# Residual in place in the image buffer, tokens as whole rows, one quarter later

## The chip, the core and the metric

The kernel runs on one core of a Trainium2 chip. The metric is the time of one execution on the device in microseconds, the median of three runs. Five engines work side by side, each with its own instruction stream: TensorE (PE in the profile; PEld is its weight load), VectorE (DVE), ScalarE (ACT), GpSimd (POOL) and SyncE (SP), which here only starts DMAs. They wait for each other through semaphores.

## What is computed

Input x has 32 images of 96 channels and 56 by 56 pixels. A clustering attention is added to x, and a quantised feed-forward network (FFN) is added to that.

```python
x = x + conv_ref(layernorm_over_channels(x), ...)
t = to_tokens(x)                       # one token per pixel, 96 channels
t = t + ffn_ref(layernorm(t), W1, b1, W2, b2)
x = from_tokens(t, x)
```

Attention works on 28 by 28 quarters of an image (a fold of 2 by 2) and 8 heads. In each quarter 16 centers are pooled, every pixel goes to its most similar center, and the centers' aggregates are spread back and projected. The FFN has 384 hidden units with sign-valued weights. Its activations are scaled by the largest absolute value of a group of six images, once for the hidden layer and once for the output. Five groups make 30 images; the last two get attention and a zero FFN output.

## The kernel before

The unit of work is the quarter: 784 pixels in seven tiles of 112. Each group of six images has 24 quarters (`GQ`). For a group the program first runs a pipeline over the quarters (attention, the token layer norm, the hidden layer for its maximum only), then a second pass (`second_pass`) that computes the FFN with the known scale. The final addition of the FFN output to the stored tokens waits for the group's second scale, so it runs during the pipeline of the next group (steps tagged `FINAL`), or in the last, short pipeline for group 4.

`pipeline` (L213) writes the same kind of list for every engine: a stage letter, a lag of 0 or 1, and a step. One round of the list is a **slot**. A stage letter is the number of quarters that the stage runs ahead: x statistics and normalisation (`X`), features and scores (`M`), assignment and output of the attention (`A`), tokens and final additions (`R`). Lag 1 means that the step runs one slot after its stage began. Since the list is written out by hand, it alone sets the order on each engine. Slots ahead of quarter 0 exist only in the first group; in all others the next group's first quarters are handled in the last slots of the group before. The last part runs over the eight quarters of images 30 and 31; its `scaled` and `finish` do three quarters of group 4 in each slot.

Data on this path:

- `xbuf` has four buffers, each one half of an image (28 rows of 56 pixels) as read from `x`. `image_rows` (L253) gives a quarter of it: 28 rows of which each has 28 of 56 numbers. Buffer j holds quarters 2j and 2j+1, side by side.
- `gather` (L498) on ScalarE copies an x quarter into `xq`.
- `residual` (L754) on VectorE adds the attention's output in PSUM, the bias and the x quarter, and writes to the staging buffer `tq` (two quarters).
- `to_tokens("t", 6)` (L900) on TensorE transposes the seven tiles of `tq`; `stats("t", 6)` follows on VectorE, `moments("t", ...)` on GpSimd.
- `place_t` (L506) on ScalarE copies `tq` over the x quarter in `xbuf`, so that SP can store whole half images.
- `scaled` (L805) multiplies a quarter of FFN output, and `finish` (L815) clips it and adds it to the stored tokens, which SP has read back into `fin` (two half images).
- On SP, `body` (L312) does for each half image: store of the previous group's final half, store of this group's half, wait for it, load of x, wait for the final store, load of the next `fin`.

`marks` (L448) on GpSimd marks the best center of every pixel; it follows `maxima` (L717) on VectorE. `newton` (L421) on GpSimd makes the inverse norms that `cosine` (L710) needs.

## Time and profile before

| | us |
|---|---|
| runs | 3263.29, 3264.39, 3267.81 (median 3264.39) |
| span of the profiled execution | 3259.8 |
| TensorE busy | 2986.8 (92%) |
| VectorE busy | 2731.3 (84%) |
| ScalarE busy | 2271.4 (70%) |
| GpSimd busy | 2034.3 (62%) |

The profiled execution is one run of the program; its span goes from its first to its last instruction and lies 4.6 us under the median. Durations below come from it. "Busy" sums the instructions of an engine, whether or not anybody waited for them; the chain of work follows the last instruction back through whatever released it.

### The profile page before, as it was taken

Reading aid. Unit: us, or ns where it says so; the run is one execution under the profiler, and the core shown is the slowest. Engines: PE = TensorE matmul, PEld = TensorE weight load, DVE = VectorE, ACT = ScalarE, POOL = GpSimd, SP = SyncE. Lnnn points to the kernel's source line nnn. Section 1 sums busy time; section 2 is a strip of 40 time slices with the busy share of each in tenths; the row PEclk is TensorE's granted clock in tenths of the full one; section 3 lists DMA queues with packets and bytes.
Section 4 is the critical chain, followed back from the end, with each engine's and each line's share of the span. In section 5 each row is a group of like instructions: output and inputs, shape, how many; then the busy total and the mean of one; then the engine's idle time right before and its main releaser. Section 6 shows DMA issues by size and latency. Waiting matters only on the chain.

```text
span 3259.8 us, 72165 instructions
## 1 busy us (share of the span) xinstructions
PE 2986.8 (92%) x20760; PEld 2046.0 (63%) x20760; DVE 2731.3 (84%) x5896; ACT 2271.4 (70%) x4628; POOL 2034.3 (62%) x4668
## 2 busy tenths in 40 slices
PE   3999999989999988999998989999988999998985
PEld 2677776666666655666665566666655666665553
DVE  3788887989988987998887978888887889897966
ACT  1677676967776787777676967767686767677943
POOL 1676675256766755777675757766655777675743
PEclk9999998999999989999998989999988999998977
DMA  1011111012222200222221012222200222120024
GB/s 47 16 31 39 38 33 31 0 45 61 61 65 57 60 16 16 61 61 68 58 64 38 0 47 68 64 58 67 60 2 16 68 68 71 52 68 23 15 72 122
DMA packets 31010, 155.43 MB, mean 48 GB/s; under 512 B 6483, under 2 KB 6676, under 8 KB 30612
## 3 DMA queue, kind: packets, MB, share of 16 engines
q1 hardware_dynamic: 30612, 150.74, 16.7%
q8 instruction: 174, 2.85, 0.4%
q14 instruction: 224, 1.84, 0.2%
HBM read 76.06 MB, written 74.66 MB: 46 GB/s over the span
## 4 chain that ended last, share of the span: by engine, by line
POOL 40%; PE 24%; issue 22%; ACT 7%; DVE 6%; POOLq 1%; ACTq 0%; DVEq 0%; SPq 0%
PE ps L958 5%; POOL eq L452 5%; POOL mo_x L397 4%; PE ps L1033 4%; POOL mo_t L397 4%; ACT turns L588 3%; PE ps L1071 3%; POOL nxy L428 3%; POOL ninv L434 3%; POOL ny L426 3%; POOL mo_x L390 2%; POOL nxy L431 2%; POOL turns L468 2%; PE ps L922 2%; PE ps L966 2%
## 5 line engine op out<-in xcount | busy, mean ns | idle before, releaser
L958 PE MATMUL ps<-wfT,xn 97*112 97x384 f32 x1792 | 734.8, 521 | 39.5 <-issue 21.5
L1033 PE MATMUL ps<-tok,w1T 98*128 (+1 forms) x2880 | 615.1, 338 | 31.8 <-ACT turns L591 29.2
L532 ACT ACTIVATE sq<-ps 112x384 f32<-112x384 f32 x896 | 432.5, 490 | 212.6 <-PE ps L958 208.4
L784 DVE TENSOR_REDUCE hmax<-ps 128x392 f32 (+1 forms) x720 | 394.7, 561 | 72.3 <-PE ps L1033 63.1
L468 POOL CAST turns<-turns 128x392 f16<-128x392 f32 x240 | 319.6, 1348 | 209.2 <-ACT turns L588 200.2
L1033 PEld LDWEIGHTS ps<-tok,w1T 98*128 98x128 f16 x2880 | 282.9, 100 | 236.7 <-issue 54.8
L958 PEld LDWEIGHTS ps<-wfT,xn 97*112 97x112 f32 x1792 | 268.1, 181 | 250.0 <-ACT sq L532 82.0
L704 DVE TENSOR_REDUCE n<-sq 112x32 f32<-112x1536 f32 (+1 forms) x256 | 394.0, 1539 | 13.6 <-issue 8.5
L493 ACT ACTIVATE xnT<-ps,mo_x 112x96 f32<-112x96 f32 x896 | 305.2, 456 | 66.5 <-POOL mo_x L399 66.5
L855 DVE SCALAR_TENSOR_TENSOR turns<-turns 128x1176 f16<-128x1176 f32 x240 | 333.9, 1391 | 0.0
L538 ACT ACTIVATE sig<-cosb,betac 112x896 f32<-112x896 f32 x128 | 133.6, 1044 | 280.1 <-DVE cosb L714 280.0
L493 ACT ACTIVATE nT<-ps,mo_t 112x96 f32<-112x96 f32 x840 | 284.8, 439 | 59.4 <-POOL mo_t L399 48.6
L588 ACT ACTIVATE turns<-ps,scale 128x1176 f32<-128x1176 f32 x240 | 312.8, 1303 | 9.1 <-PE ps L1033 4.8
L1071 PE MATMUL ps<-turns,w2T 128*96 128x392 f16 x1440 | 292.5, 341 | 22.9 <-DVE turns L855 20.1
L452 POOL TENSOR_TENSOR eq<-sig,top 112x896 bf16<-112x896 f32 x128 | 219.8, 1717 | 116.2 <-issue 61.0
L966 PE MATMUL ps<-Q,xn 97*112 97x128 f32 x1792 | 240.5, 288 | 48.7 <-issue 25.5
L922 PE MATMUL ps<-cst,xnT 112*97 112x128 f32 x1792 | 254.5, 284 | 17.6 <-ACT xnT L493 17.6
L922 PEld LDWEIGHTS ps<-cst,xnT 112*97 112x97 f32 x1792 | 219.7, 168 | 66.3 <-ACT xnT L493 47.6
L966 PEld LDWEIGHTS ps<-Q,xn 97*112 97x112 f32 x1792 | 212.9, 184 | 68.1 <-ACT sq L532 36.9
L1071 PEld LDWEIGHTS ps<-turns,w2T 128*96 128x96 f16 x1440 | 164.2, 125 | 136.4 <-DVE turns L855 53.1
L998 PE MATMUL ps<-sim,xnT 112*97 112x128 f32 x1792 | 229.5, 281 | 2.4 <-ACT turns L554 2.3
L776 DVE TENSOR_TENSOR tok<-ps,tok 98x448 f32 (+1 forms) x240 | 135.8, 566 | 109.9 <-ACT tok L565 103.5
(130 smaller groups left out, 6369.3 us busy)
## 6 DMA issues: line engine op xcount, KB each, us to landing
xbuf<-in_x SPq DMA_DIRECT2D x64, 588.0 KB, 4.7
out<-xbuf SPq DMA_DIRECT2D x64, 588.0 KB, 3.7
turns<-out SPq DMA_DIRECT2D x60, 588.0 KB, 6.2
out<-turns SPq DMA_DIRECT2D x60, 588.0 KB, 3.7
cst<-in_constants SPq DMA_DIRECT2D x1, 644.0 KB
tok<-in_L_ffn_W SPq DMA_DIRECT2D x2, 142.5 KB
wf<-in_L_conv_Wf SPq DMA_DIRECT2D x1, 144.0 KB
tok<-in_L_conv_Wv SPq DMA_DIRECT2D x1, 144.0 KB
```

What stands on the lines that cost most here:

```text
L452: nc.gpsimd.tensor_tensor(heads(eq[:, :]), heads(sig[:, k % 2, :]), over_centers(top[:, :]), ALU.subtract)\
L468: nc.gpsimd.tensor_copy(ghi[:, k % 3, HT:2 * HT], gel[:, k % 3, HT:2 * HT]).then_inc(b_mid, 1)
L493: ins = nc.scalar.activation(dst, bank(b0 + part, TN, C, (t - t0) * C), ACT.Identity, bias=m[:, 9, t:t + 1], scale=m[:, 8, t:t + 1])
L532: nc.scalar.activation(sq[:, t, :], bank(2 + t % 2, TN, D), ACT.Square).then_inc(f_sq, 1)
L588: nc.scalar.activation(gel[:, k % 3, :].rearrange("p (c n) -> p c n", c=FC), ps[:, h:h + 3, 0:HT], ACT.Gelu, scale=scale[:, 0:1]).then_inc ...
L704: ins = v.reduce_sum(n2[:, t0 * HEADS:t1 * HEADS], sq[:, t0:t1, :].rearrange("p t (h d) -> p (t h) d", d=HD), AX.X)
L784: v.tensor_reduce(o, bank(6 + u % 2, 128, HT), AX.X, ALU.max, apply_absolute_value=True)\
L922: ins = mm(bank(part, C + 1, BN, (t - t0) * BN), xnT[:, k % 4, t, :], backm[:, t, :], start=True, stop=True)
L958: mm(bank(2 + t % 2, TN, D), xn[:, k % 2, t * TN:(t + 1) * TN], wfT[:, :], start=True, stop=True)\
L966: ins = mm(tile_bank(2, TN, HM, t), xn[:, k % 2, t * TN:(t + 1) * TN], Q[:, k % 2, :], start=True, stop=True)
L1033: ins = mm(dst, w1T[:, c * 128:(c + 1) * 128], tok[:, bass.ds(place, 1), part, s * HT:(s + 1) * HT].rearrange("p a n -> p (a n)"), start=p ...
L1071: ins = mm(bank(6 + k % 2, C, HT), w2T[:, c, :], part[:, s, c * HT:(c + 1) * HT], start=n == 0, stop=n == 2 * FC - 1)
```

## The change

`residual` writes its sum to the place in `xbuf` from which it read x. `tq`, `place_t` and the semaphore `t_placed` are gone, and with them the waits of `residual` for the copy and for the transposes of two quarters before. The transposes read `xbuf`: token quarter k is no longer the 28 by 28 square of the attention but 14 whole rows of the half image, 784 consecutive numbers. Such a quarter needs both squares of its half, so `to_tokens` waits for the residual of the odd quarter in both cases, and the stages X, M and A run one quarter further ahead (4, 3, 2). The FFN output has the same token order, so `finish` adds consecutive numbers too. SP stores a half when its residual is done, and loads the next x over it when it has been transposed as well.

```diff
-        X, M, A, R = 3, 2, 1, 0
+        X, M, A, R = 4, 3, 2, 0
@@ SP, body
-                    done(sp, "t_placed", g * GQ + b * BODY + (2 * j + 1))
+                    done(sp, "t_done", g * GQ + b * BODY + (2 * j + 1))
                     store(image, j)
                     sp.wait_ge(t_out[j], (g * BODIES + b) * 16 + 16)
                     sp.sem_inc(waited, 1)
+                    done(sp, "t_T", g * GQ + b * BODY + (2 * j + 1))
                     load(x_half, image + XB // 2, j)
@@ ScalarE, attention
-                        (X, 1, normalise("x", 0, 1)), (R, 1, place_t), (X, 1, copy_x(0)), (X, 1, copy_x(1)),
+                        (X, 1, normalise("x", 0, 1)), (X, 1, copy_x(0)), (X, 1, copy_x(1)),
@@ VectorE, residual
-                    if half == 0:
-                        done(dve, "t_placed", q - 2)
-                        if part != "last":
-                            done(dve, "t_T", q - 2)
                     o = bank(4 + half, C, hi - lo).rearrange("c (r w) -> c r w", w=QS)
-                    t = tq[:, k % 2, lo:hi].rearrange("c (r w) -> c r w", w=QS)
-                    ins = v.scalar_tensor_tensor(t, o, bpc[:, :], image_rows(k, lo // QS, (hi - lo) // QS), ALU.add, ALU.add)
+                    t = image_rows(k, lo // QS, (hi - lo) // QS)
+                    ins = v.scalar_tensor_tensor(t, o, bpc[:, :], t, ALU.add, ALU.add)
@@ VectorE, finish
-                    t = fin[:, k // 2 % 2, :].rearrange("c (r w) -> c r w", w=SIDE)[:, :, k % 2 * QS:(k % 2 + 1) * QS]
-                    v.scalar_tensor_tensor(t, y_of(place).rearrange("c (r w) -> c r w", w=QS), -QCLIP, t,
-                                           ALU.max, ALU.add).then_inc(S["final"], 1)
+                    t = fin[:, k // 2 % 2, k % 2 * QN:(k % 2 + 1) * QN]
+                    v.scalar_tensor_tensor(t, y_of(place), -QCLIP, t, ALU.max, ALU.add).then_inc(S["final"], 1)
@@ TensorE, to_tokens
-                        done(pe, "t_done", q)
+                        done(pe, "t_done", q + 1 - k % 2)
                         pe.wait_ge(h_max, q * (2 * FC) + START)
                     for t in range(T):
-                        src = (xq if s == "x" else tq)[:, k % 2, t * TN:(t + 1) * TN]
+                        if s == "x":
+                            src = xq[:, k % 2, t * TN:(t + 1) * TN]
+                        else:
+                            src = xbuf[:, k // 2, k % 2 * QN + t * TN:k % 2 * QN + (t + 1) * TN]
```

How VectorE comes from `cosine` to the maxima in a full slot. First before: `tq` is the target of the residual, and the semaphores that an instruction waits for stand in brackets.

```order
L714 TENSOR_TENSOR cosb<-ps,ninv 112x896 [waits s_sig_done,s_n_newton3,s_s_ps]
L678 TENSOR_TENSOR cbd<-ps,cst 96x128 [waits s_q_ps,s_cen_f]
L765 SCALAR_TENSOR_TENSOR tq<-ps,bpc,xbuf 96x448 [waits s_t_T,s_t_placed,s_o_ps0]
L784 TENSOR_REDUCE hmax<-ps 128x1 [waits h_ps]
L765 SCALAR_TENSOR_TENSOR tq<-ps,bpc,xbuf 96x336 [waits s_o_ps]
```

The same stretch after the change:

```order
L708 TENSOR_TENSOR cosb<-ps,ninv 112x896 [waits s_sig_done,s_n_newton3,s_s_ps]
L672 TENSOR_TENSOR cbd<-ps,cst 96x128 [waits s_q_ps,s_cen_f]
L755 SCALAR_TENSOR_TENSOR xbuf<-ps,bpc,xbuf 96x16x28 [waits s_o_ps0]
L774 TENSOR_REDUCE hmax<-ps 128x1 [waits h_ps]
L755 SCALAR_TENSOR_TENSOR xbuf<-ps,bpc,xbuf 96x12x28 [waits s_o_ps]
```

The instructions stand in the same order; the target is `xbuf` in rows of 28, and two waits are gone.

The end of VectorE's stream, the last slots of the last part. Before: `rden` to `aggp` and the residual L765 belong to the last quarter's attention, L811 is the scaling, L821 the final addition.

```order
L738 RECIPROCAL rden<-ps 128x1 [waits s_a_ps]
L742 TENSOR_SCALAR hmul<-cst,rden 128x2 [waits s_a_rden]
L746 TENSOR_SCALAR a<-ps,hmul 128x96 [waits s_a_mul]
L751 SCALAR_TENSOR_TENSOR aggp<-ps,hmul,a 128x96 [waits s_o_ps,s_a_half]
L765 SCALAR_TENSOR_TENSOR tq<-ps,bpc,xbuf 96x448 [waits s_t_placed,s_o_ps0]
L765 SCALAR_TENSOR_TENSOR tq<-ps,bpc,xbuf 96x336 [waits s_o_ps]
L811 TENSOR_SCALAR tok<-tok,scale 96x784 x3
L821 SCALAR_TENSOR_TENSOR turns<-tok,turns 96x28x28 [waits s_c_min]
L821 SCALAR_TENSOR_TENSOR turns<-tok,turns 96x28x28 [waits s_c_min,f_in1]
L821 SCALAR_TENSOR_TENSOR turns<-tok,turns 96x28x28 [waits s_c_min]
```

After (L801 is the scaling, L811 the final addition):

```order
L755 SCALAR_TENSOR_TENSOR xbuf<-ps,bpc,xbuf 96x16x28 [waits s_o_ps0]
L755 SCALAR_TENSOR_TENSOR xbuf<-ps,bpc,xbuf 96x12x28 [waits s_o_ps]
L801 TENSOR_SCALAR tok<-tok,scale 96x784 x3
L811 SCALAR_TENSOR_TENSOR turns<-tok,turns 96x784 [waits s_c_min,f_in1]
L811 SCALAR_TENSOR_TENSOR turns<-tok,turns 96x784 [waits s_c_min]
L811 SCALAR_TENSOR_TENSOR turns<-tok,turns 96x784 [waits s_c_min,f_in0]
L801 TENSOR_SCALAR tok<-tok,scale 96x784 x3
L811 SCALAR_TENSOR_TENSOR turns<-tok,turns 96x784 [waits s_c_min]
L811 SCALAR_TENSOR_TENSOR turns<-tok,turns 96x784 [waits s_c_min,f_in1]
L811 SCALAR_TENSOR_TENSOR turns<-tok,turns 96x784 [waits s_c_min]
```

The last residual now stands ahead of six final additions instead of three; `f_in0` and `f_in1` are the loads of the two `fin` buffers.

The start of TensorE's stream, from the spread of the first quarter's attention (L1016, after it L1008) to the marks' transposes (L975, after it L967). Before:

```order
L1016 MATMUL ps<-turns,aggp 96x336 [waits s_a_done]
L958 MATMUL ps<-wfT,xn 112x384 [waits s_xn_copied0,s_cos_done]
L938 MATMUL ps<-cst,csq 128x1 [waits s_cen_sq,s_cen_bd]
L941 MATMUL ps<-wf,cbd 32x97 x4
L958 MATMUL ps<-wfT,xn 112x384
L911 MATMUL ps<-cst,tq 112x96 [waits h_max,s_t_done]
L911 MATMUL ps<-cst,tq 112x96 x6
```

After:

```order
L1008 MATMUL ps<-turns,aggp 96x336 [waits s_a_done]
L950 MATMUL ps<-wfT,xn 112x384 [waits s_xn_copied0,s_cos_done]
L930 MATMUL ps<-cst,csq 128x1 [waits s_cen_sq,s_cen_bd]
L933 MATMUL ps<-wf,cbd 32x97 x4
L950 MATMUL ps<-wfT,xn 112x384
L950 MATMUL ps<-wfT,xn 112x384 [waits f_sq] x2
L939 MATMUL ps<-cst,qT 97x128 [waits s_q_scaled]
```

The token transposes are missing in this slot and come one slot later, from `xbuf`.

## Rows read from the trace of the kernel before

**Rows 1.** Chain of work, middle slots of group 1: start us, us, what.
```profile
795.25 1.71 POOL eq L452
...
814.46 1.72 POOL eq L452
...
831.22 0.67 DVE tq L765
...
832.37 0.47 DVE tq L765
```

**Rows 2.** Timeline of one middle slot: start us, us, engine, line, operation [idle before].
```profile
807.02 0.86 ACT L509 COPY xbuf<-tq 96x784 f32<-96x784 f32 x1
...
808.83 0.44 ACT L522 COPY xn<-ps 97x336 f32<-97x336 f32 x1 [0.53 <-PE ps L922]
...
810.50 1.09 DVE L714 TENSOR_TENSOR cosb<-ps,ninv 112x896 f32<-112x896 f32 x1 [0.59 <-issue]
...
812.77 0.56 DVE L765 SCALAR_TENSOR_TENSOR tq<-ps,bpc,xbuf 96x336 f32<-96x336 f32 x1
...
813.73 0.74 PE L911 MATMUL ps<-cst,tq 96*112 96x96 f32 x7
```

**Rows 3.** Timeline of VectorE, first slots: the x statistics.
```profile
92.34 1.25 DVE L661 BATCH_NORM_STATS2 st_x<-ps 112x6 f32<-112x96 f32 x7
...
110.74 1.25 DVE L661 BATCH_NORM_STATS2 st_x<-ps 112x6 f32<-112x96 f32 x7 [0.20 <-PE ps L911]
...
129.17 1.25 DVE L661 BATCH_NORM_STATS2 st_x<-ps 112x6 f32<-112x96 f32 x7 [0.20 <-PE ps L911]
```

**Rows 4.** Timeline of VectorE, last part: final additions of slots three to eight.
```profile
3149.26 2.73 DVE L821 SCALAR_TENSOR_TENSOR turns<-tok,turns 96x784 f32<-96x784 f32 x3
...
3175.18 2.73 DVE L821 SCALAR_TENSOR_TENSOR turns<-tok,turns 96x784 f32<-96x784 f32 x3
...
3196.58 2.73 DVE L821 SCALAR_TENSOR_TENSOR turns<-tok,turns 96x784 f32<-96x784 f32 x3
...
3216.82 2.73 DVE L821 SCALAR_TENSOR_TENSOR turns<-tok,turns 96x784 f32<-96x784 f32 x3
...
3235.98 2.73 DVE L821 SCALAR_TENSOR_TENSOR turns<-tok,turns 96x784 f32<-96x784 f32 x3
...
3245.64 1.69 DVE L811 TENSOR_SCALAR tok<-tok,scale 96x784 f32<-96x784 f32 x3
3247.25 2.73 DVE L821 SCALAR_TENSOR_TENSOR turns<-tok,turns 96x784 f32<-96x784 f32 x3
```

**Rows 5.** Timeline of SP's queue, last part: issues of DMAs.
```profile
3227.78 0.32 SPq L301 DMA_DIRECT2D turns<-out  x1
...
3248.24 4.04 SPq L306 DMA_DIRECT2D out<-turns  x2
3255.69 0.32 SPq L297 DMA_DIRECT2D out<-xbuf  x1
```

**Rows 6.** Groups of instructions: busy us, mean ns of one, idle before and releaser.
```profile
L855 DVE SCALAR_TENSOR_TENSOR turns<-turns 128x1176 f16<-128x1176 f32 x240 | 333.9, 1391 | 0.0
...
L765 DVE SCALAR_TENSOR_TENSOR tq<-ps,bpc,xbuf 96x448 f32<-96x448 f32 (+1 forms) x256 | 156.4, 613 | 2.0 <-PE ps L1016 2.0
...
L821 DVE SCALAR_TENSOR_TENSOR turns<-tok,turns 96x784 f32<-96x784 f32 x120 | 113.9, 959 | 0.0
L509 ACT COPY xbuf<-tq 96x784 f32<-96x784 f32 x128 | 110.6, 864 | 6.8 <-DVE tq L765 6.8
```

**Rows 7.** Timeline of GpSimd, last part: an instruction beneath three final additions.
```profile
3149.30 2.77 POOL L390 TENSOR_SCALAR mo_x<-mo_x 112x7 f32<-112x7 f32 x1
```

**Rows 8.** From 3175 us on: landing of the six `fin` loads, then of eight final stores.
```profile
DMA to landing us min/median/max: 4.4/4.6/4.7
...
DMA to landing us min/median/max: 3.6/3.7/5.8
```

**Rows 9.** The page's first line.
```profile
span 3259.8 us, 72165 instructions
```

More of the change, by code:

```diff
@@ L504, in gather @@
                     .then_inc(S["x_side"], 1)
-            def place_t(k, q, place, use):
-                done(act, "t_done", q)
-                nc.scalar.copy(image_rows(k), tq[:, k % 2, :].rearrange("c (r w) -> c r w", w=QS))\
-                    .then_inc(S["t_placed"], 1)
             def copy_x(part):
@@ L752, in second_heads, with residual @@
                     .then_inc(S["a_done"], 1)
-            def residual(half, part):
+            def residual(half):
                 _, _, lo, hi, end = BANKS[half]
@@ L832, in attention @@
                          (R, 1, h_largest(2, 3), FFN), (A, 1, second_heads), (R, 1, h_largest(3, 5), FFN),
-                         (X, 1, pooled), (M, 1, cosine), (X, 1, centers), (A, 1, residual(0, part)),
-                         (R, 1, h_largest(5, 6), FFN), (A, 1, residual(1, part)), (X, 1, center_floor),
+                         (X, 1, pooled), (M, 1, cosine), (X, 1, centers), (A, 1, residual(0)),
+                         (R, 1, h_largest(5, 6), FFN), (A, 1, residual(1)), (X, 1, center_floor),
                          (A, 0, maxima), (X, 1, q_scaled), (R, 0, stats("t", 6), FFN),
```

5 lines of the change are left out of this document (2 added, 3 removed).

## The prediction, made before the change was run

> **What bounds the kernel now.** I read the chain of work first, then the timeline of one slot of a middle group, then the two ends of the program. A slot is one round of the hand-written order, which each engine runs once per quarter of an image. In a middle group the slots follow each other every 19.21 us: GpSimd's `marks` starts at 795.25 and again at 814.46 [rows 1]. Between them the chain stays on GpSimd until its third Newton step ends; VectorE takes over at 810.50 with `cosine` [rows 2] and keeps it for 4 us: the centers, the two halves of the residual with one `h_largest` between them (831.22 and 832.37 in the next slot, [rows 1]), the maxima, and then GpSimd again. So GpSimd and VectorE close a ring. TensorE is the busiest engine but not on it, and neither is ScalarE. 96 of the 120 full slots are of this kind. In group 0, where no final additions run, a slot takes 18.43 us (110.74 to 129.17, [rows 3]). At the end, eight slots carry the last eight quarters together with the 24 outstanding final additions, three in each [rows 4], and a run of DMAs closes the program [rows 5].
>
> **The staging copy.** ScalarE loses 128 copies of 864 ns, 110.6 us of its busy time [rows 6]. In a middle slot the copy stands at 807.02, before the two copies of xn; the second of those then waits 0.53 us for TensorE until 808.83 [rows 2]. The removed 0.86 us becomes idle time in front of a copy that TensorE releases. What hides it is the x-back matmuls, and nothing of it is on the ring: 0. Were that cover gone, it would be worth up to the 110.6 us; the wait at 808.83 excludes that.
>
> **The residual in place.** This is the one edited instruction on the ring, twice per slot. It reads strided rows of the image buffer already and now writes them too, 28 of every 56 numbers. It takes 613 ns on average for a mean of 392 elements [rows 6]. No such instruction of before writes so from PSUM; the nearest is the final addition L821, which reads and writes strided rows: 959 ns for 784 elements, 1.22 ns each. The contiguous L855 takes 1391 ns for 1176, 1.18 ns each [rows 6]. If all of that difference were the stride it would be 3%, 0.02 us an instruction, 0.04 us a slot, 4 us over 96 slots; since a shorter instruction carries more fixed time per element, I take 0 and keep 4 us to each side. The two waits that leave it (for the copy and the transposes of two slots before) were long met: 0.
>
> **The wait of the transposes.** For an even quarter `to_tokens` now waits for the residual of the next quarter. That residual is computed in the same slot, since its lead grew by one, so the event comes at the same place: VectorE ends it at 813.33, TensorE begins at 813.73 [rows 2]. Behind the wait on TensorE stand the feature matmuls and, through them, ScalarE's squares; with a margin of 0.4 us nobody waits. Odd quarters find their residual done a slot ago, but TensorE gets to them in its own order and no earlier. 0 for both.
>
> **Final additions on whole rows.** The same elements, now contiguous: 959 ns stays, down to 927 by L855's rate. While L821 runs, GpSimd stands: in the last stage one small GpSimd instruction lasts 2.77 us [rows 7] beneath three of them at 3149.26 [rows 4]. [...]
>
> **SP's queue.** In middle groups SP waited for ScalarE's copy, one slot after the final addition; now the x store goes out right behind the final store, and the next load waits for the transposes, which precede that addition on VectorE. A store lands after 3.7 us, 5.8 at most, a load after 4.6 [rows 8]: some 12 us together, and the gather needs them two slots (38 us) later. Behind SP's new wait stand only the next half's DMAs. 0.
>
> **The pipeline is one slot deeper.** The leads go from 3, 2, 1 to 4, 3, 2. In middle groups this only renames quarters. At the start there is one more slot of attention before the FFN begins. X statistics start at 92.34, 110.74 and 129.17 [rows 3]; the new slot has the work of the one from 92.34 to 110.74, 18.40 us, without its seven token transposes (0.74 us on TensorE, [rows 2]). The feature matmuls behind those also wait for ScalarE's squares, so I take nothing off: **+18.4 us**, lower bound 17.7.
>
> At the end one slot of full attention goes. The first three periods have the same work in both kernels, so the one that goes is the fourth, 3175.18 to 3196.58: **-21.4 us** [rows 4]. Its three final additions do not go; they land in a last slot that has nothing else. Call T the start of the additions in the slot before the one with the last residual. Before, T = 3235.98; the last slot starts its own at T+11.27, its first is done at T+12.2 [rows 4], and three stores in series from 3248.24 to 3255.69 and 3.7 us more [rows 5] end at T+23.8. After, T lies in the sixth slot. In the seventh the third addition needs an input half whose load goes out 10.96 us after T (3227.78 against 3216.82, [rows 4, 5]) and lands 4.6 us later [rows 8]: it runs from T+15.6 to T+16.6. Three scalings (1.69 us together, [rows 4]) and the first addition of the eighth slot end at T+19.2. The store of half 9 could go at T+13.2 but stands behind a load and a store of x, so I estimate its landing at T+18.6; the last input half is there at T+23.3, two additions end at T+25.2, the last final store at T+29.0, the last x store at T+32.8, the program at **T+33.2**: **+9.4 us**. Bounds: +4.3 if no load were late (first addition T+16.5, then the same 11.6); +14 if every transfer on the way took 5.8.
>
> **The sum.** 18.4 - 21.4 + 9.4 = **+6.4 us**. The profiled execution spans 3259.8 us [rows 9]; the median of the runs, 3264.39, is 4.6 above it. That makes a span of 3266.2 and a median of 3270.8, 0.20% more. A measurement of this kernel can tell about 0.2% (6.5 us) from no change, so the forecast lies just inside that line.
>
> **The rivals.**
> *Shorter slots (faster).* Fewer ScalarE instructions and fewer waits on VectorE draw 0.15 us out of each ring: -14.4 + 6.4, so 3256.4. For it: the ring has gaps of some tenths between instructions; against: none of them lies at an edited wait. Chance 0.1, and half of it at smaller gains.
> *Whole rows make the final addition faster.* The scaling of a whole quarter takes 0.56 us when GpSimd is silent (1.69 for three, [rows 4]). If L821 did as well, GpSimd would be free 0.40 us earlier in 96 slots: -38 us, 3232.4. L855, contiguous and with two inputs, speaks against it with 1.18 ns an element. The Trainium skill (VectorE: DVE Perf Modes, The perf-mode tier table) gives two-tensor fp32 instructions only the single rate; the trace agrees. Chance 0.02.
> *The last loads hold up one more slot (slower).* If final additions wait for input in the sixth slot as well, a load's 4.6 us is added: 3275.4. It decides as soon as two sets of additions follow within the 15.6 us that a store and a load take. Periods of 19 us and more speak against it before the seventh slot. Chance 0.18.
> *The clock at the end.* The third period took 25.92 us instead of 21.4 (3149.26 to 3175.18, [rows 4]). If the shortened end loses or gains such a slot, it moves 4.5 us: 3266.3 or 3275.3. Chance 0.2, split evenly.
>
> **How the numbers follow.** The forecast itself keeps 0.5; 0.17 of that lies past the 0.2% line, since its own unknowns are some 4 us to each side. Slower by over 0.2%: 0.18 + 0.1 + 0.17 = 0.45. Faster by over 0.2%: 0.08 of the first two rivals, the rest of them falls within. Within: 0.47. The range goes from 3260, where the small gains of the first rival end, to 3276, past the two slower rivals.
>
> **What would show it.** In the profile after, ScalarE is some 110 us less busy, and two `marks` of a middle slot stay 19.2 us apart. The first FFN matmul comes 18.4 us later. In the last stage seven slots carry attention, the last two sets of final additions wait for loads, and SP's last stores no longer stand back to back. A middle slot that is off by 0.1 us moves the whole by 10 us and breaks the forecast, and so would a residual above 0.65 us on average.

## The result: 22 us faster, where 6 us slower was predicted

| | before, same chip | after |
|---|---|---|
| median of four runs | 3266.03 | 3243.77 |
| runs | 3263.29 to 3267.81 | 3240.04 to 3246.68 |
| span of the profiled execution | 3259.8 | 3244.8 |

The ratio of the runs is 0.9934, with a 95% interval of 0.992 to 0.9948. The predicted range began at 3260. The sign was wrong. The profiled execution of the changed kernel was its slowest run (3246.68), so the two spans differ by 15.0 us only; the stretches below are taken from them.

The page of the changed kernel, its first lines:

```profile
span 3244.8 us, 71952 instructions
...
PE 2979.5 (92%) x20760; PEld 2041.8 (63%) x20760; DVE 2709.1 (83%) x5896; ACT 2176.7 (67%) x4500; POOL 1858.7 (57%) x4668
```

ScalarE is 95 us less busy, near the 110 of the copy. Part of the rest is in the second passes, where its activations are recorded longer (L588 before, L582 after: 1303 and 1497 ns on average) though they follow each other no more slowly. GpSimd lost 176 us, though the change does not touch one instruction of it. That is the first thing that the prediction has no term for.

The lines that answer to [rows 1], chain of work of the changed kernel in the middle slots of group 1 (start us, us, what), two `marks` of neighbouring slots:

```profile
796.37 1.71 POOL eq L452
815.59 1.72 POOL eq L452
```

They stand 19.22 us apart, as in [rows 1]. Timeline of the same slot, the lines that answer to [rows 2]: residual (L755, L765 before) and token transposes (L903, L911 before).

```profile
812.83 0.67 DVE L755 SCALAR_TENSOR_TENSOR xbuf<-ps,bpc,xbuf 96x448 f32<-96x448 f32 x1
813.89 0.56 DVE L755 SCALAR_TENSOR_TENSOR xbuf<-ps,bpc,xbuf 96x336 f32<-96x336 f32 x1
...
814.86 0.74 PE L903 MATMUL ps<-cst,xbuf 96*112 96x96 f32 x7
```

The residual ends at 814.45 and the transposes begin 0.41 us later, as before. By the page of the changed kernel, stores from `xbuf` land after 5.7 us instead of 3.7 and final stores after 4.4 instead of 3.7; no slot got longer by it. The groups of instructions that answer to [rows 6], and three of the second pass (busy us, mean ns of one):

```profile
L844 DVE SCALAR_TENSOR_TENSOR turns<-turns 128x1176 f16<-128x1176 f32 x240 | 333.4, 1389 | 0.0
...
L755 DVE SCALAR_TENSOR_TENSOR xbuf<-ps,bpc,xbuf 96x448 f32<-96x448 f32 (+1 forms) x256 | 156.4, 613 | 1.6 <-PE ps L1008 1.6
L468 POOL CAST turns<-turns 128x392 f16<-128x392 f32 x240 | 143.3, 597 | 367.4 <-ACT turns L582 358.5 <-PE ps L1063 8.9
...
L811 DVE SCALAR_TENSOR_TENSOR turns<-tok,turns 96x784 f32<-96x784 f32 x120 | 113.9, 958 | 7.4 <-DMA turns<-out 7.4
L837 DVE CAST turns<-turns 128x392 f16<-128x392 f32 x240 | 86.3, 360 | 27.3 <-ACT turns L582 23.2 <-PE ps L1063 2.4
```

And the two that moved, in the kernel before:

```profile
L468 POOL CAST turns<-turns 128x392 f16<-128x392 f32 x240 | 319.6, 1348 | 209.2 <-ACT turns L588 200.2 <-PE ps L1071 9.0
...
L848 DVE CAST turns<-turns 128x392 f16<-128x392 f32 x240 | 109.0, 454 | 26.1 <-ACT turns L588 23.0 <-PE ps L1071 2.6
```

The residual in place costs what it cost (613 ns), and the final addition on whole rows too (958 ns). But GpSimd's cast of the second pass, an instruction that nobody edited, went from 1348 to 597 ns.

To see where the time went, both executions are cut at the start of GpSimd's first and the end of its last cast of each second pass (48 casts in each):

| stretch | before | after | difference | predicted |
|---|---|---|---|---|
| start to first cast of group 0 | 564.1 | 584.1 | +20.0 | +18.4 |
| four first passes, groups 1 to 4 | 2007.9 | 2001.5 | -6.4 | 0 |
| five second passes | 512.6 | 494.5 | -18.1 | 0 |
| last cast to the end | 175.2 | 164.7 | -10.5 | -12.0 |
| span | 3259.8 | 3244.8 | -15.0 | +6.4 |

The head, and the tail as a whole, are as predicted within 1.6 us. What it called unchanged is not.

**The second pass.** For each tile of 392 tokens, VectorE and GpSimd each cast a third of the hidden layer's output (L848 and L468 before), and VectorE takes the rest after subtracting (L855, two inputs in SBUF). Before, the pass takes 99.2 us in group 0 and 103.6, 103.0, 103.2 and 103.5 us in groups 1 to 4; after, 98.3 to 99.3 in all five. Timeline of the kernel before, group 1, around the tenth cast (in brackets the idle time of the engine ahead):

```profile
1178.87 0.35 DVE L848 CAST turns<-turns 128x392 f16<-128x392 f32 x1
1179.01 0.59 POOL L468 CAST turns<-turns 128x392 f16<-128x392 f32 x1 [1.44 <-ACT turns L588]
...
1181.33 2.07 POOL L468 CAST turns<-turns 128x392 f16<-128x392 f32 x1 [1.73 <-ACT turns L588]
...
1181.65 1.37 DVE L855 SCALAR_TENSOR_TENSOR turns<-turns 128x1176 f16<-128x1176 f32 x1
...
1182.96 0.66 DVE L848 CAST turns<-turns 128x392 f16<-128x392 f32 x1
```

A cast follows the last by 2.03 us. This one follows by 2.32, so it is 0.29 us late. It has not ended when VectorE starts L855, and it ends only after L855 does: 2.07 us instead of 0.59. Such a cast is called caught below. VectorE's next cast L848 then runs beneath it and takes 0.66 us instead of 0.35, the next L855 starts 2.36 us after the last one, and the pass never gets back in step. From the fifteenth cast on, every second one is slow, at 2.9 to 3.1 us, as the twelfth is already:

```profile
1185.20 2.86 POOL L468 CAST turns<-turns 128x392 f16<-128x392 f32 x1 [1.21 <-ACT turns L588]
```

In all, 19 of the 48 casts take over 1 us in each of the four passes, and in all four it begins at the tenth. VectorE's tiles then take 2.03 and 2.35 us in turn, 2.19 on average, against 2.08 in an undisturbed pass: over 38 tiles that is the 4 us that a slow pass costs. The Trainium skill (SBUF — State Buffer, Who interferes with whom) states that a VectorE instruction with two SBUF inputs contends with a GpSimd instruction that reads SBUF, and that the order of issue decides who is blocked. The trace agrees that both engines lose (2.07 for 0.59, 0.66 for 0.35); it does not bear out that the one that issued first keeps going, since the cast had begun 0.32 us before L855 and was the one to be stretched, while L855 kept its 1.37 us.

The same stretch of the changed kernel, tenth cast of group 1:

```profile
1199.17 0.59 POOL L468 CAST turns<-turns 128x392 f16<-128x392 f32 x1 [1.44 <-ACT turns L582]
1199.78 1.37 DVE L844 SCALAR_TENSOR_TENSOR turns<-turns 128x1176 f16<-128x1176 f32 x1
```

The cast ends 0.02 us before the two-input instruction begins. There is no late one.

**What makes the tenth cast late?** In the DMA view of the kernel before, from 1181 to 1183 us there is one packet, and it carries instructions:

```profile
DMA packets 1, 0.01 MB, mean 4 GB/s; under 512 B 0, under 2 KB 0, under 8 KB 0
...
q14 instruction: 1, 0.01, 1.6%
```

Such a packet (8 KB) starts 0.64 to 0.66 us behind the start of the late cast in each of the four passes. So the first theory was: when GpSimd's stream runs into a new packet, one instruction is late, and where that happens depends on how many instructions stand ahead. The deeper pipeline adds some to GpSimd's first, unrolled slots, and so shifts every later one. **Theory A** is that this place decides. **Theory B** is that the SBUF addresses do, which moved when `tq` went. **Theory C** is that the in-place residual or the new order acts on the second pass.

**The tail**, which answers to [rows 4] and [rows 5]. Timeline of VectorE, scalings and final additions of the last slots:

```profile
3211.10 2.73 DVE L811 SCALAR_TENSOR_TENSOR turns<-tok,turns 96x784 f32<-96x784 f32 x3
...
3227.06 0.97 DVE L811 SCALAR_TENSOR_TENSOR turns<-tok,turns 96x784 f32<-96x784 f32 x1 [2.90 <-DMA turns<-out]
3227.96 1.70 DVE L801 TENSOR_SCALAR tok<-tok,scale 96x784 f32<-96x784 f32 x3
...
3235.08 1.85 DVE L811 SCALAR_TENSOR_TENSOR turns<-tok,turns 96x784 f32<-96x784 f32 x2 [4.54 <-DMA turns<-out]
```

T is 3211.10. The third addition of the seventh slot waits for a load and runs from T+16.0 (predicted T+15.6), the last two wait for another and end at T+25.8 (T+25.2), and the program ends at T+33.7 (T+33.2).

### The profile page after: what moved, and what is told of

The parts are those of the page before. It is cut to its first block, busy times and chain, and to the rows that moved or that the text cites. A ratio compares the mean times of both kernels' runs of the same rounds, so it can differ in the third digit from the quotient of the medians.

```text
span 3244.8 us, 71952 instructions
## 1 busy us (share of the span) xinstructions
PE 2979.5 (92%) x20760; PEld 2041.8 (63%) x20760; DVE 2709.1 (83%) x5896; ACT 2176.7 (67%) x4500; POOL 1858.7 (57%) x4668
## 4 chain that ended last, share of the span: by engine, by line
POOL 40%; PE 31%; issue 22%; DVE 3%; ACT 2%; POOLq 1%; DMA 0%; DVEq 0%; ACTq 0%; SPq 0%
PE ps L1025 9%; PE ps L1063 7%; POOL eq L452 5%; POOL mo_x L397 5%; PE ps L950 5%; POOL mo_t L397 4%; POOL nxy L428 3%; POOL ninv L434 3%; POOL ny L426 3%; POOL nxy L431 2%; POOL mo_x L390 2%; PE ps L914 2%; PE ps L958 2%; POOL cinv L441 1%; POOL mo_t L380 1%
## 5 line engine op out<-in xcount | busy, mean ns | idle before, releaser
L582 ACT ACTIVATE turns<-ps,scale 128x1176 f32<-128x1176 f32 x240 | 359.2, 1497 | 8.6 <-PE ps L1025 5.0
L468 POOL CAST turns<-turns 128x392 f16<-128x392 f32 x240 | 143.3, 597 | 367.4 <-ACT turns L582 358.5
L958 PE MATMUL ps<-Q,xn 97*112 97x128 f32 x1792 | 238.0, 287 | 40.2 <-ACT sq L526 23.2
L914 PE MATMUL ps<-cst,xnT 112*97 112x128 f32 x1792 | 252.4, 283 | 15.7 <-ACT xnT L493 14.6
L516 ACT COPY xn<-ps 97x448 f32<-97x448 f32 (+1 forms) x256 | 124.4, 486 | 160.5 <-PE ps L914 160.2
```

Of the source, the lines that this page charges most:

```text
L582: nc.scalar.activation(gel[:, k % 3, :].rearrange("p (c n) -> p c n", c=FC), ps[:, h:h + 3, 0:HT], ACT.Gelu, scale=scale[:, 0:1]).then_inc ...
L914: ins = mm(bank(part, C + 1, BN, (t - t0) * BN), xnT[:, k % 4, t, :], backm[:, t, :], start=True, stop=True)
L958: ins = mm(tile_bank(2, TN, HM, t), xn[:, k % 2, t * TN:(t + 1) * TN], Q[:, k % 2, :], start=True, stop=True)
```

## Experiments

The stretches of every profiled execution, cut as above. A pass is called slow when more than ten of its 48 casts take over 1 us (19 in those of the kernel before). Undisturbed middle slots differ by some 0.03 us between executions, 3 us over 96 slots, so differences of a few us between rows carry no weight. The ratio is to the kernel before on the same chip, with its 95% interval.

| kernel | ratio | head | first passes | second passes | slow | tail | span |
|---|---|---|---|---|---|---|---|
| before | | 564.1 | 2007.9 | 512.6 | 4 | 175.2 | 3259.8 |
| after | 0.9934 (0.9920 to 0.9948) | 584.1 | 2001.5 | 494.5 | 0 | 164.7 | 3244.8 |
| e1_before_29 | 0.9938 (0.9918 to 0.9957) | 563.9 | 2001.8 | 498.9 | 1 | 171.5 | 3236.2 |
| e2_after_99 | 0.9943 (0.9924 to 0.9961) | 579.4 | 2000.7 | 491.7 | 0 | 165.2 | 3237.0 |
| e3_before_128 | 0.9996 (0.9984 to 1.0008) | 564.4 | 2007.7 | 510.5 | 4 | 176.8 | 3259.4 |
| e4_leads_only | 0.9946 (0.9927 to 0.9965) | 582.1 | 2000.8 | 491.7 | 0 | 160.8 | 3235.3 |
| e5_before_40 | 0.9959 (0.9946 to 0.9972) | 565.3 | 2011.2 | 491.6 | 0 | 172.1 | 3240.3 |
| e6_cast_first | 1.0115 (1.0100 to 1.0131) | 564.5 | 2007.6 | 547.5 | 5 | 175.5 | 3295.1 |
| e7_after_again | 0.9953 (0.9941 to 0.9966) | 579.9 | 1999.8 | 492.8 | 0 | 161.7 | 3234.1 |
| e8_leads_again | 0.9940 (0.9928 to 0.9952) | 586.1 | 2001.2 | 494.4 | 0 | 162.5 | 3244.2 |
| e9_after_unrolled | 0.9830 (0.9813 to 0.9846) | 582.0 | 1964.5 | 493.8 | 0 | 164.2 | 3204.5 |
| e10_third_buffer | 0.9943 (0.9926 to 0.9959) | 583.5 | 1998.2 | 493.9 | 0 | 157.2 | 3232.8 |
| e11_both | 0.9812 (0.9795 to 0.9828) | 580.6 | 1968.2 | 493.6 | 0 | 155.7 | 3198.1 |
| e12_before_unrolled | 0.9885 (0.9870 to 0.9900) | 560.1 | 1972.5 | 510.8 | 4 | 176.3 | 3219.6 |
| e13_unrolled_again | 0.9840 (0.9827 to 0.9854) | 579.3 | 1968.5 | 490.3 | 0 | 164.5 | 3202.7 |
| e14_before_clean | 0.9855 (0.9838 to 0.9871) | 568.5 | 1967.8 | 493.3 | 0 | 172.5 | 3202.0 |
| e15_unrolled_third | 0.9840 (0.9824 to 0.9855) | 581.4 | 1967.9 | 493.3 | 0 | 164.3 | 3207.0 |

### The place of GpSimd's code: e1, e2, e3

The edit, at the start of GpSimd's stream, with 29 and 128 in the kernel before and 99 in the changed one:

```diff
             pool.wait_ge(pool_set, POOL_SETS)
+            for _ in range(29):
+                pool.sem_inc(waited, 1)
```

> The kernel before with 29 semaphore increments that nobody waits for, at the start of GpSimd's stream; all else as it is. They bring GpSimd's second-pass loop of the middle groups from instructions 1290 to 1302 of its stream to 1319 to 1331, where the changed kernel has it. Theory A (the place of GpSimd's code): 35 or 36 slow casts in each middle second pass come from an instruction fetch that falls into the tenth cast; here it falls elsewhere, the passes take 99 us as in the changed kernel, and the run takes some 18 us less than before: 3248. Theory B (the SBUF addresses, which moved when the staging buffer went) and theory C (something that the pipeline or the in-place residual does to the second pass): nothing of either is here, so 3266 and four passes of 103.4 us.

> The changed kernel with 99 such increments at the start of GpSimd's stream. They put the second-pass loop of the middle groups at 1418 to 1430, exactly 128 instructions behind its place in the kernel before. An instruction packet of GpSimd is 8 KB; that 128 instructions fill one is an assumption of this run. Theory A: the slow casts come back in four passes, +18 us, about 3262. Theories B and C: 3244 as without the 99.

> The kernel before with 128 such increments: a control for the first run. The second-pass loop stands at the same place of an instruction packet as before, one packet later. Theory A: the four passes stay slow, 3266. If instead any added instruction removed the slow casts, 3248.

**e1** is the decisive run: nothing but 29 idle instructions more, and the kernel before is as fast as the changed one (3238.15 against 3257.96 on that chip). Theories B and C are not needed for the slow passes, since neither the addresses nor the order nor the residual changed. But it did not go quite as theory A said. One cast is late in each middle pass still, now the second. Timeline of e1, group 1, the second and third casts:

```profile
1160.20 1.38 DVE L857 SCALAR_TENSOR_TENSOR turns<-turns 128x1176 f16<-128x1176 f32 x1
...
1160.34 1.61 POOL L470 CAST turns<-turns 128x392 f16<-128x392 f32 x1 [1.29 <-ACT turns L590]
...
1162.47 0.61 POOL L470 CAST turns<-turns 128x392 f16<-128x392 f32 x1 [0.52 <-ACT turns L590]
```

It is 0.29 us late and caught (1.61 us), but there the engines still wait for ScalarE and TensorE to fill the pipeline, and in three of four passes they fall back into step at the third cast. In group 4 they do not, and that pass takes 104.2 us.

**e3**, the control, is the kernel before again: four slow passes from the tenth cast on, ratio 0.9996. So added instructions as such do nothing, and 128 of them bring the late cast back to its place. The Trainium skill (Runtime: NRT & Kernel Launch, Instruction fetch mechanics) gives 512 instructions to 32 KiB; by that figure 128 of them would make an 8 KB packet, an estimate with which the period in e3 agrees. The section has refills of 16 KiB whose crossing is "mostly hidden"; here one instruction is some 0.3 us late at each of the places in question.

**e2** missed. The slow casts did not come back (0.9943), although a late one did: in all five passes the seventh cast starts 0.35 us late.

```profile
1185.27 0.58 POOL L470 CAST turns<-turns 128x392 f16<-128x392 f32 x1 [1.49 <-ACT turns L584]
...
1187.69 0.51 POOL L470 CAST turns<-turns 128x392 f16<-128x392 f32 x1 [1.84 <-ACT turns L584]
...
1188.10 1.37 DVE L846 SCALAR_TENSOR_TENSOR turns<-turns 128x1176 f16<-128x1176 f32 x1
```

This cast starts 0.41 us before the two-input instruction, not 0.32, and overlaps it by 0.10 us only. That is not enough to be caught. And the place was wrong because the count behind 29 and 99 left out instructions that set registers. With them, GpSimd's second-pass loop of the middle groups starts at these instructions of its stream:

| kernel | loop starts at | from before | late cast |
|---|---|---|---|
| before | 1851 | 0 | tenth, caught |
| e1 | 1880 | 29 | second, caught, three of four recover |
| e5 | 1891 | 40 | none |
| after, e4 | 1892 | 41 | none |
| e3 | 1979 | 128 | tenth, caught |
| e2 | 1991 | 140, or 12 past 128 | seventh, not caught |

One count orders all six kernels. The late instruction itself stands directly ahead of the cast or two ahead of it. Counted among the records of the trace, each loop body once, it is number 1860 in before and e1 and number 1988, 128 further, in e2 and e3; in the changed kernel, e4 and e5 neither number falls into a second pass. (These numbers run some five below those of the table.) The late one in group 0 of e2 is number 1092, seven steps of 128 below 1988. For group 0 of the kernel before, one more step gives 964, an instruction of the ninth cast: it is recorded 0.28 us late, at 581.90, but the cast, at 581.62, is not. Why the cast isn't late there stays open; the loop of group 0 stands one instruction off (956 instead of 955, by steps of 128).

What the runs show is the place and the period. That the engine waits for the packet is inferred from them and from the packet behind each late instruction. Besides, no run put slow casts back into the changed kernel, where e2 was meant to.

### Which part of the change shifts the code: e4, e8

```diff
-        X, M, A, R = 3, 2, 1, 0
+        X, M, A, R = 4, 3, 2, 0
```

> The kernel before with the leads 4, 3, 2 alone; staging buffer, copy and final additions on squares stay. GpSimd's stream is then that of the changed kernel, instruction by instruction. Theory A: the second passes run at 99 us, head +20 and tail -10.5 as in the changed kernel, so 3244 to 3248; what is left to the changed kernel is what the staging copy and the in-place residual are worth (0 by the prediction). Theories B and C (addresses, or the copy and in-place writes): passes stay at 103.4 us, +9.5 us against before, 3275.

> The kernel with the leads 4, 3, 2 alone again, beside the others. Theory A2 with the prediction's terms: equal to the changed kernel within 4 us, since the staging copy and the in-place residual were taken at 0. Rival B2: 4 us or more slower than the changed kernel, by the 110 us that ScalarE no longer spends on the staging copy.

Ratios 0.9946 and, on another chip, 0.9940, against 0.9934 and 0.9953 of the changed kernel. The leads alone have the whole effect. The staging copy, the in-place residual, the new waits and the whole rows together are worth 0 within some 6 us, by the intervals of e7 and e8 on one chip (medians 3251.24 and 3245.36; e8 was expected within 4 us of e7). The prediction had 0 for them, though ScalarE still spends 110.4 us on the copy in e8:

```profile
L509 ACT COPY xbuf<-tq 96x784 f32<-96x784 f32 x128 | 110.4, 863 | 7.6 <-DVE tq L765 7.6
```

### The kernel before without any late cast: e5, beside e7

The edit is that of e1 with 40.

> The kernel before with 40 idle increments at the start of GpSimd's stream instead of 29. With 0 of them the late cast was the tenth of each middle second pass, with 29 the second; each cast takes some three instructions of the stream, so 40 bring it ahead of the first cast. Theory A2 (a cast that starts 0.3 us late because of a fetch is caught under VectorE's L855, and the pass then stays slow): five passes of 98 to 99 us, none slow, 20 us less than before; ratio 0.994 (3246 against 3266), a little under that of the changed kernel: the prediction's +6.4 us should remain between this kernel and the changed one. Rival B2 (the changed order and the in-place residual have a gain of their own): the changed kernel is as fast as this one or faster.

> The changed kernel, beside the others on one chip. Ratio 0.993 as measured. Theory A2: 3 to 7 us over the kernel with 40 increments (the prediction's +6.4). Rival B2: not over it.

No pass is slow. The ratio, 0.9959, beside 0.9953 of the changed kernel on the same chip: the two are equal within some 6 us. So the whole measured gain of the change can be had without it. It is less than the 0.994 expected, because the shift also moved stalls of 0.3 us into eight slots of each first pass (19.48 to 19.50 us from `marks` to `marks` instead of 19.20); the kernel before has one such slot in each, the changed kernel four. The first passes take 2011.2 us against 1999.8 in e7: 5 us of the difference are such stalls, and 6 us lie in the slots of the jump (below). Neither A2's +6.4 nor a gain can be told from this pair.

### A wait against being caught: e6

```diff
+                def cast_first(k, i, place):
+                    dve.wait_ge(b_mid, i + (START + 1))
...
-                second_pass(dve, g, [(0, first_chunk), (4, y_largest), (1, low_parts)])
+                second_pass(dve, g, [(0, first_chunk), (4, y_largest), (0, cast_first), (1, low_parts)])
```

> The kernel before with one edit on VectorE alone: in the second pass L855 of tile i-1 also waits for GpSimd's cast of tile i, which in an undisturbed tile has ended 0.02 us before it anyway. GpSimd's stream is unchanged, so the tenth cast should start 0.3 us late as before. Theory A2: it is no longer caught, VectorE waits once for 0.3 us, and the passes stay at 99 to 101 us: 14 to 18 us less than before, ratio 0.995. If the slow passes came from the code's place alone and not from the two instructions running together, nothing changes: ratio 1. If the new wait falls on the ring of the pass, 0.05 us more in each of 240 tiles: at most +12 us on top.

This failed: 1.0115, all five passes 109 to 110 us. Timeline of e6, group 2, L858 of the sixth tile and the casts of the eighth:

```profile
1798.03 0.56 DVE L863 TENSOR_REDUCE ymax<-tok  x1
1798.71 1.38 DVE L858 SCALAR_TENSOR_TENSOR turns<-turns 128x1176 f16<-128x1176 f32 x1
1799.88 0.58 POOL L468 CAST turns<-turns 128x392 f16<-128x392 f32 x1 [1.46 <-ACT turns L588]
1800.01 0.67 DVE L848 CAST turns<-turns 128x392 f16<-128x392 f32 x1
```

The wait holds L858 of the sixth tile until GpSimd's seventh cast has ended, before any cast is late: it starts 0.68 us behind L863, where L855 before starts 0.48 behind L860. That is enough for GpSimd's next cast to come 0.13 us ahead of VectorE's L848, which runs beneath it and takes 0.67 us instead of 0.36. From there on L848 is that slow in every tile, and the period is 2.35 us, with no idle time on VectorE. In an undisturbed tile GpSimd's cast ends 0.02 us before L855 starts; a wait between them has no room. The run says that the overlap costs time wherever it comes from, and that this wait doesn't remove it but brings it about, in group 0 too.

### The slot with the jump: e9

In each group one slot is long. Timeline of GpSimd, changed kernel, `marks` of group 1:

```profile
970.00 1.72 POOL L452 TENSOR_TENSOR eq<-sig,top 112x896 bf16<-112x896 f32 x1 [0.43 <-DVE top L713]
989.25 1.72 POOL L452 TENSOR_TENSOR eq<-sig,top 112x896 bf16<-112x896 f32 x1 [0.42 <-DVE top L713]
1016.18 1.72 POOL L452 TENSOR_TENSOR eq<-sig,top 112x896 bf16<-112x896 f32 x1 [0.42 <-DVE top L713]
```

It takes 26.93 us, its neighbours 19.25. In groups 1 to 4 it takes 27.82, 26.99, 27.62 and 27.39 us before and 26.93, 26.45, 24.19 and 26.03 after, together 6.2 us less: nearly all that the first passes gained. This goes with the leads and not with the place of GpSimd's code: the four slots together take 108.7 to 110.9 us in the kernels with leads 3, 2, 1 (before, e1, e3, e5, e6) and 101.0 to 103.6 in those with 4, 3, 2 (after, e2, e4, e7, e8, e10). It is the slot in which the inner loop of `pipeline` jumps back. After the jump three engines wait for nothing that the profile shows:

```profile
997.72 3.32 PE L958 MATMUL ps<-Q,xn 97*112 97x128 f32 x14 [3.69 <-issue]
998.14 1.08 ACT L493 ACTIVATE nT<-ps,mo_t 112x96 f32<-112x96 f32 x3 [2.06 <-issue]
998.22 0.21 POOL L380 TENSOR_TENSOR mo_x<-st_x 112x7 f32<-112x7 f32 x1 [3.57 <-issue]
```

The granted clock (PEclk, after the engines' busy times) of the slot before and of this one:

```profile
972.00:991.00 19.00, 18.64 (x142) 13.10 (x141) 17.09 (x42) 13.03 (x30) 13.48 (x36) 1.00 0.01 2
991.00:1018.00 27.00, 22.86 (x143) 17.55 (x141) 17.41 (x42) 13.49 (x31) 13.19 (x36) 0.81 0.34 93
```

It is at its upper level (2.4 GHz) before, and part of the long slot at the lower one (1.2 GHz), in which TensorE stood still for 3.69 us. The edit:

```diff
-            with eng.Fori(1, BODIES) as b:
+            for b in range(1, BODIES):
                 slots(range(BODY), b, lambda n, d: True)
```

> The changed kernel with the two inner rounds of each group's pipeline written out instead of looped, on all engines that run it. In every group one slot takes 24 to 28 us where its neighbours take 19.2: it is the one in which the loop jumps back. Theory A2 (what moved the time between the kernels is where the instruction streams jump and are fetched): that slot falls to 19.5 us in all five groups, 7 us less in each middle group and 6 in the first, 34 us together: 3210 against 3244, ratio to before 0.983. GpSimd's code moves too, so a late cast may appear in the second passes: caught, it would give back up to 20 us. If the slow slot has another cause (the clock, or a wait for a DMA), nothing changes: 3244.

Measured: 3200.55, ratio 0.983, and `marks` of group 1 at the same place:

```profile
985.58 1.71 POOL L452 TENSOR_TENSOR eq<-sig,top 112x896 bf16<-112x896 f32 x1 [0.42 <-DVE top L713]
1004.76 1.71 POOL L452 TENSOR_TENSOR eq<-sig,top 112x896 bf16<-112x896 f32 x1 [0.43 <-DVE top L713]
1023.95 1.71 POOL L452 TENSOR_TENSOR eq<-sig,top 112x896 bf16<-112x896 f32 x1 [0.42 <-DVE top L713]
```

The slot is an ordinary one of 19.2 us, and no pass is slow. Against e10, which ran on the same chip with the loops, the first passes of groups 1 to 4 are 34 us shorter: 26 us of it in the four slots of the jump (27.11, 24.36, 26.78 and 24.76 us in e10), some 4 us in stalls of 0.3 us that are gone; the rest was not followed up. In group 0 the slot is ordinary too (18.4 us instead of 23.2 in e10), yet the head is only 1.5 us shorter than in e10, where 6 were expected; 2.7 us are lost in the first slots (fourth `marks` at 149.0 instead of 146.3). The jump was the cause of the long slot. The Trainium skill (Runtime: NRT & Kernel Launch, Instruction fetch mechanics) says that a taken branch out of the window makes the engine fetch before it can go on, and that kernels prefer full unrolling for it; the gain of e9 agrees.

### A third buffer at the end: e10, e11

In the last part a third half-image buffer `fx`, in the room of `tq`:

```diff
+        fx = sb("fx", [C, HALF])
+        def last_half(h):
+            return fx[:, :] if h % 3 == 2 else fin[:, h % 3, :]
@@ SP, last part
-                store_final(GROUPS, b, j)
-                final_stored(GROUPS, b, j)
-                if h + 2 < XB * BODIES:
-                    load_t(GROUPS * GSIZE - GSIZE + b * (XB // 2), j + 2)
+                sp.dma_start(half(o_half, GROUPS * GSIZE - GSIZE, h), last_half(h)).then_inc(l_out[h % 3], 16)
+                if h + 3 < XB * BODIES:
+                    sp.wait_ge(l_out[h % 3], (h // 3 + 1) * 16)
+                    load_last(h + 3)
```

The edit also takes the waits out from between the last stores and sends the last x store ahead of the last two final ones.

> The changed kernel with a third buffer for half images in the last part (in the room that the staging buffer left), so that the last final additions no longer wait for loads, with no wait between the last stores and with the last x store ahead of the last two final stores. The prediction put the program's end 33.2 us after T, the additions of the slot before the one with the last residual; in its term +9.4 us are the late loads. With them gone: the first addition of the eighth slot ends at T+16.5, the last one at T+18.5, the last store lands at T+23 to T+25, 9 us less than the changed kernel: 3235, ratio to before 0.991. If something other than loads ends the program (the chain of stores), 4 us less at most.

> Both edits together. Theory A2: the sum, 43 us less than the changed kernel: 3201, ratio to before 0.980, if no cast of the second passes is caught; 3220 if they are.

Timeline of e10, VectorE's last additions and SP's last store:

```profile
3206.80 0.96 DVE L831 SCALAR_TENSOR_TENSOR turns<-tok,turns 96x784 f32<-96x784 f32 x1
...
3223.21 1.85 DVE L831 SCALAR_TENSOR_TENSOR fx<-tok,fx 96x784 f32<-96x784 f32 x2
```

```profile
3225.09 0.87 SPq L359 DMA_DIRECT2D out<-fx  x1
```

No addition waits for a load. The last two end at T+18.3 (expected 18.5) and the program at T+26.0 (3232.8), 7.7 us before the changed kernel's T+33.7 and a little over the 23 to 25 expected. Since 7.5 of the 7.7 us are there when the last addition ends, it is the loads that made the tail longer and not the stores, as the prediction's term of +9.4 us had it. The runs alone (0.9943) can't tell 8 us of this from the changed kernel's 0.9934 and 0.9953.

**e11** has both edits: 3196.42 us, ratio 0.9812, beside 3256.92 for the kernel before. Expected were 3201 and 0.980. It is the fastest kernel of the study, 1.2 to 1.4% below the changed one by the ratios.

### The change by itself: e12 to e15

e12 is the kernel before with the unrolled rounds of e9 and the 29 increments of e1. e13 and e15 are e9 again. e14 has these edits to the kernel before:

```diff
-            with eng.Fori(1, BODIES) as b:
+            for b in range(1, BODIES):
@@ GpSimd
+            for _ in range(39):
+                pool.sem_inc(waited, 1)
@@ VectorE
+            for _ in range(114):
+                dve.sem_inc(waited, 1)
```

> The kernel before with the inner rounds of the pipeline written out and 29 idle increments at the start of GpSimd's stream, which put its middle second pass where the unrolled changed kernel has it. Against that kernel only the change itself is left. If the prediction's terms hold (+18.4 at the head, -12.0 at the tail), this one is 6.4 us faster than the unrolled changed kernel: ratio to before 0.981 against 0.983. If the change has a gain of its own, it is slower: 0.985 or more. With a caught cast in each pass it would be some 20 us slower than either says.

> The unrolled changed kernel again, beside the other. Ratio to before 0.983 as measured; head 18 to 20 us longer than in the other, tail 10 to 12 us shorter, the rest equal within 2 us.

e12 fits neither account: 0.9885, with four slow passes. No cast of GpSimd is late this time. Timeline of e12, group 1:

```profile
1164.63 0.35 DVE L850 CAST turns<-turns 128x392 f16<-128x392 f32 x1
...
1165.14 0.56 DVE L862 TENSOR_REDUCE ymax<-tok  x1
...
1166.79 0.58 POOL L470 CAST turns<-turns 128x392 f16<-128x392 f32 x1 [1.43 <-ACT turns L590]
...
1166.90 0.68 DVE L850 CAST turns<-turns 128x392 f16<-128x392 f32 x1
...
1168.86 2.88 POOL L470 CAST turns<-turns 128x392 f16<-128x392 f32 x1 [1.50 <-ACT turns L590]
```

Here VectorE is late. L862 follows L850 by 0.51 us where it is 0.27 to 0.35 elsewhere, an instruction packet starts 0.67 us behind it as with GpSimd's late casts, and so GpSimd's cast (1166.79) comes ahead of VectorE's (1166.90), which runs beneath it for 0.68 us. One tile later GpSimd's cast is caught. Either engine can start it; what counts is that VectorE's cast and its two-input instruction keep their places around GpSimd's cast. Against e12, e13 has a head that is 19.2 us longer and a tail that is 11.8 us shorter, both as expected; the rest was expected equal within 2 us and is 24.5 us shorter, 20.5 of it in the slow passes.

> The kernel before with the inner rounds of the pipeline written out, 39 idle increments at the start of GpSimd's stream and 114 at the start of VectorE's. By a count that now includes the register instructions, GpSimd's second-pass loop of the middle groups starts at instruction 2695 as in the unrolled changed kernel, and VectorE's at 3106, 128 behind that kernel's 2978. Theory A3 (an instruction fetch of either engine that falls into a second pass makes one instruction late; the two engines' casts change places, and the pass stays slow): no slow pass, 20 us less than the unrolled kernel before without the increments on VectorE, 3201 against 3221, and 3 to 7 us less than the unrolled changed kernel, ratio to before 0.982. Rival (the change is what keeps the passes fast, whatever the places): four slow passes, ratio 0.988.

> The unrolled changed kernel a third time, as the partner. Ratio to before 0.984; 3 to 7 us over the other by theory A3 with the prediction's head and tail.

With both streams in the same place modulo 128, no pass of the kernel before is slow, and the two kernels agree between head and tail: 1967.8 and 1967.9 us of first passes, 493.3 and 493.3 us of second passes. That they do so to 0.1 us is luck, since e9, e13 and e15, one kernel, differ by 4 us in either. Theory A3 forecast the passes without a slow one; it rests on this one run. The medians are 3208.56 and 3206.88, ratios 0.9855 and 0.9840, which intervals of 0.0016 to each side don't tell apart. e14 was expected to be 3 to 7 us faster and is not. Its 114 increments stand where VectorE starts its work and lengthen the head by 8.4 us (560.1 in e12, 568.5 in e14); without them it would stand at 3200, 7 us under its partner. That last figure is worked out, not measured.

## Why the prediction was wrong, step by step

- **The staging copy, the residual in place, the wait of the transposes, whole rows, SP's queue: 0 each. Right.** e4 and e8 have the copy and none of the other edits and are as fast. 613 and 958 ns are unchanged, and the middle slots stay at 19.22 us.
- **The head: +18.4. Right.** It measured +20.0, +19.2 between e12 and e13, and +14.6 between e5 and e7. In the changed kernel the x statistics start at 92.11, 110.38 and 130.44: the new slot itself takes 18.27 us, as predicted, and the 1.6 us above it are in the next one, 20.06 us instead of 18.43.
- **The tail: -21.4 + 9.4 = -12.0. Right.** It measured -10.5, and -11.8 between e12 and e13. From the last cast to T it is 151.4 us before and 131.0 after, -20.4 for the predicted -21.4, and T+33.7 stands for the predicted T+33.2. The rival *the last loads hold up one more slot* did not come about.
- **"In middle groups this only renames quarters." This step failed.** By it the deeper pipeline cost or gave nothing between head and tail. It is true of the work and of the slots' order, and the second pass was not looked at since no line of it was edited. But the instructions of group 0's longer start stand ahead of all later ones. They shifted GpSimd's loop by 41 instructions and took its late cast out of the second passes: -18.1 us. The jump's slot became shorter too, as in every kernel with the new leads: -6.2 us. Neither had a term, and together, against the 3 us by which head and tail came out longer than forecast, they turned +6.4 into the measured result of -15.0 in the profiled executions.
- **The rival *shorter slots* gave the right sign for a reason that was wrong.** No slot of the ring got shorter, apart from that of the jump.
- What could have shown it: GpSimd's cast at 1348 ns against a smallest of 510, four passes of 103 us beside one of 99, all four slow from the same cast on. The trace of before held the 18 us; it was a cost of the kernel before that hung on a margin of 0.02 us. A forecast could have named it as a rival: *any edit that moves code may end it*.
- What the change itself costs, without places: head and tail together +9.5 (before and after), +7.4 (e12 and e13), +13 (e14 and e15, the increments taken off), +4.1 (e5 and e7). The prediction's +6.4 lies among them. With the loops in place, the shorter slot of the jump pays for about all of it, and e5 and e7 measure alike.

Two things stay open. One is why the jump's slot is shorter with leads of 4, 3 and 2: its clock and its fetches differ from group to group and were not separated. The other is why many 8 KB instruction packets that start in a second pass go with no slow cast: at 17 to 19 us in e4 and e8, and at 20.6 to 22.0 us in e9, e11, e13, e14 and e15. So such a packet alone predicts nothing.

## What to carry to other kernels

Before an edit is credited or blamed, compare the stretches it does not touch: a group of instructions whose mean doubled without an edit, or one pass slower than its twins, is a state of the schedule and not of the work. Where two engines slow each other down and pass each other with no slack, a few idle instructions at the start of a stream are a cheap test of whether such a state hangs on the place of the code. And a loop whose body is some hundreds of instructions pays for each jump back; here writing it out was worth 34 us in four groups, more than the change under study.

## What the runs showed of the hardware

- One instruction starts 0.24 to 0.35 us late, on GpSimd or on VectorE, in every iteration of the outer loop, and an 8 KB packet of instructions starts 0.54 to 0.69 us behind it (before, e1, e2, e3, e12). On GpSimd its place has a period of 128 instructions (e1, e2, e3). That a fetch is the cause is inferred.
- A GpSimd cast of 0.59 us that overlaps a two-input VectorE instruction by a quarter of a microsecond takes 2.07 us (before, e3), and the disturbance keeps itself alive: from there on every second cast takes 2.9 to 3.1 us, and a tile 2.19 us instead of 2.08 on average (before). With 0.10 us of overlap it does not start (e2).
- A jump back over a long loop body costs 5 to 9 us in one slot (24.19 us in after, 28.42 in e3, instead of 19.2): 2 to 4 us of issue on three engines, and a mean granted clock of 0.81 in that slot (after, group 1). All of it goes when the loop is written out (e9).
